# Graph layers by one-hot matmuls: 64 columns in two column groups instead of 32 columns in four

## The chip, the core and the metric

The kernel runs on one NeuronCore of a Trainium2 chip. Its engines are TensorE (PE; its weight loads are listed apart as PEld), VectorE (DVE), ScalarE (ACT), GpSimd (POOL) and SyncE (SP), which run side by side and wait for each other by semaphores. The metric is the device time of one execution in microseconds (us), as the median of several runs.

## The reference

A graph has 3125 nodes with 768 features and 50,000 edges, sorted by their target node. Two layers follow each other, each on a normalised copy of its input and each added to it:

```python
h = relu(layernorm(x)); x = x + conv(relu(conv(h, W1, b1)), W2, b2)   # D^-1/2 (A + I) D^-1/2 h W^T + b
h = relu(layernorm(x)); x = x + attention(h)                          # 12 heads of 64 features
# attention, per head: ft = h W_fc^T; e = leaky(a1[src] + a2[dst]); alpha = softmax of e over the edges of one dst
# relu(sum over edges of alpha * ft[src]  +  h W_res^T)
```

In each of the three passes over the edges (two convolutions, one attention) a node receives the sum of the rows of its source nodes, in attention weighted by alpha.

## The kernel before

**Tiles and gathers.** The nodes are 25 tiles of 128 (the last has 53), and a tile has four units of 32 nodes. The edges of a tile come in quads. A quad holds 17 chunks of 128 edges: four chunks for each unit (512 edges), and one extra chunk whose 128 places are shared by the units. With this input every tile has one quad; the last tile has two units, so a pass makes 24 x 17 + 9 = 417 gathers. A gather is one indirect DMA that POOL issues: it fetches 128 rows (3 KB each, in attention a little more) of a table in DRAM to the 128 partitions of one chunk.

**Sums by one-hots.** For a chunk, DVE makes a 128 x 32 matrix with a one where the edge (partition) goes to the node (column). PE takes it as the stationary operand and the chunk's rows as the moving one, and accumulates in PSUM. As the one-hot has 32 columns, `add` (line 777, matmul at line 779) cuts the 768 features into four strips of 192, each sent to its own group of 32 columns of the array, and so to its own 32 partitions of PSUM: `block_of(par, s, g)` holds for unit s the strip g on partitions 32g to 32g+31. All operands are float32, and each such matmul appears in the trace as two instructions with a weight load each. So a chunk is 8 matmul instructions and a unit 32.

**A convolution** (function `convolution`, run twice). There is one set of 17 chunk buffers, `ring_c`. POOL's `fetch` waits before the four gathers of unit s until PE has used that unit's buffers for the tile before (`unit_done[s]`), and ACT's `next_slot` hands it the row numbers. PE's `step(j)` does, for tile j, the units 0 to 3 as their rows land, the extra chunk (into `ps_x` in natural order of nodes, lines 798), and then the product of tile j-1 with the 768 x 768 weights (line 808, 24 matmul instructions). DVE, for tile j: makes the next one-hots when PE is done with the old ones (lines 833, 836), adds ACT's copy `natural` to the four strips of the four units (16 adds, line 854), waits for the product of tile j-1 (which still reads `sum_t`), transposes in blocks of 32 into `sum_t` (2 transposes, line 860), clears the PSUM half, and finishes tile j-1 (line 875 or 879, 881). Two halves of `ps_sum` alternate between tiles.

**Attention.** Here two sets of chunk buffers alternate, and the order of a tile on each engine is this.
- ACT: `cast_hot` copies the tile's one-hots (bf16) to float32 `hot_f` (line 1344, waits until PE is done with the tile before: `used[3]`); the exponentials that are the edge weights (1368 and 1372, wait for PE's transposes of the scores, line 1472); smaller copies; 36 of 48 scalings of unit 3's rows (line 1388); `sloped` for the next tile (line 1336, waits for PE's `scores`, which end in line 1462); the other 12 scalings; `lay` of the tile before (line 1354): 16 copies of 32 partitions x 192 that bring the result `o` from its strips to natural order in `ps_n`.
- DVE: scales the rows of units 0, 1 and 2 (line 1651, one operation each), between units 1 and 2 takes the terms of the next tile's scores (1562), scales the extra chunk (1658), adds the result of two tiles ago (1580), makes one-hots (1556), then runs the maxima and scans for the next tile (1613 to 1622), then `divide` (1568 to 1574, waits for `used[3]` and, for `o`, for `lay`).
- PE: units 0 and 1 (line 1493, 32 instructions each, each after its scaling), `scores` of the next tile (1455 to 1462), unit 2, the extra chunk for each unit (line 1508, 32 instructions), unit 3 (needs ACT's scalings), transposes, `natural` (the residual product, line 1420).
- POOL: gathers for the tile after next, unit by unit as `used[s]` allows.

When a tile had a second quad, a rescaling of the sums would run; with this input it doesn't.

## Time and profile before

| | |
|---|---|
| time of the runs | median 1934.79 us of 3 (1933.72 to 1936.58) |
| profiled execution, span from first to last instruction | 2277.0 us |
| PE busy | 1621.1 us, 71% |
| POOL busy | 1232.7 us, 54% |
| DVE busy | 1121.9 us, 49% |
| ACT busy | 718.1 us, 32% |
| gathers of the first convolution | begin at 112.2 us |
| gathers of attention | 1531.7 to 2226.3 us |
| mean granted TensorE clock | 0.840 of full |

The page gives no time for what lies around the span of the profiled execution. Its span alone is 342 us longer than the median of the runs, so the profiled execution is not paced as the timed ones are; the rows below have to be read with that in mind. Busy shares are averages over the stages: the part up to 112 us sorts the edges into quads, two convolutions follow, then a dense stage that prepares attention, then attention.

### The profile page before, as it was taken

How to read it: one execution, taken by the hardware profiler on the slowest of the kernel's cores; microseconds unless marked ns; L12 is line 12 of the kernel's file. 1: busy time of each engine (PE TensorE's matmuls, PEld its weight loads, DVE VectorE, ACT ScalarE, POOL GpSimd, SP SyncE). 2: the span in 40 equal slices, each digit the busy share in tenths (PEclk: the TensorE clock that was granted, in tenths of full speed). 3: DMA queues.
4: the chain of work that ended last, by engine and by line, in shares of the span. 5: the costliest groups of instructions: out<-in, count | busy, mean ns of one | idle time of the engine just before them, and what ended most of it. 6: DMA issues, size and time to landing. Idle time of an engine off the chain costs nothing. (4 is left out here: it accounts for less than half of the span.)

```text
span 2277.0 us, 43588 instructions
## 1 busy us (share of the span) xinstructions
PE 1621.1 (71%) x13579; PEld 962.8 (42%) x13580; DVE 1121.9 (49%) x2027; ACT 718.1 (32%) x2184; POOL 1232.7 (54%) x1297
## 2 busy tenths in 40 slices
PE   7337888887778858787788887882666666666665
PEld 7223444444344424344444444671334444444443
DVE  6613334333334314444444444653666666666666
ACT  6400111111111101000000100262666666777675
POOL 2166566566656266566666666106555555555550
PEclk9969888899988869798988888986787777878877
DMA  4698888888878387788787887388788888888882
GB/s 183 218 315 269 268 266 271 274 265 277 275 264 270 125 279 270 261 270 277 262 274 266 266 275 274 122 310 280 245 279 267 270 267 272 273 273 272 273 276 84
DMA packets 139992, 585.22 MB, mean 257 GB/s; under 512 B 30616, under 2 KB 32752, under 8 KB 139946
## 3 DMA queue, kind: packets, MB, share of 16 engines
q0 software_dynamic: 100272, 497.49, 65.7%
q1 hardware_dynamic: 32563, 67.72, 8.6%
q10 hardware_dynamic: 7110, 19.43, 2.2%
q8 instruction: 25, 0.41, 0.1%
q14 instruction: 22, 0.17, 0.0%
HBM read 534.42 MB, written 50.12 MB: 257 GB/s over the span
## 5 line engine op out<-in xcount | busy, mean ns | idle before, releaser
L667 POOL DMA_INDIRECT ring_c<-table,slot_c x834 | 798.1, 957 | 545.9 <-issue 268.5
L1243 POOL DMA_INDIRECT ring<-table,slot x417 | 410.4, 984 | 288.5 <-issue 105.8
L833 DVE TENSOR_TENSOR hots<-iota,units 128x256 f32<-128x256 bf16 x102 | 43.3, 426 | 602.4 <-remote 332.9
L1493 PE MATMUL ps_acc<-ring,hot_f 128*32 128x195 f32 x3136 | 230.8, 386 | 138.2 <-issue 84.4
L1388 ACT ACTIVATE ring<-ring,weight x1152 | 281.5, 340 | 0.6
L1651 DVE TENSOR_TENSOR ring<-ring,ps_w 128x3120 f32 x72 | 244.7, 3398 | 16.5 <-issue 8.9
L1493 PEld LDWEIGHTS ps_acc<-ring,hot_f 128*32 128x32 f32 x3136 | 123.9, 125 | 227.7 <-issue 124.2
L808 PE MATMUL ps_ya<-weights,sum_ta 128*128 128x512 f32 (+1 forms) x576 | 204.1, 503 | 12.5 <-issue 10.9
L808 PE MATMUL ps_yb<-weights,sum_tb 128*128 128x512 f32 (+1 forms) x576 | 196.7, 494 | 6.1 <-issue 5.5
L711 ACT ACTIVATE slot_c<-units 128x8 int32 (+1 forms) x104 | 21.7, 211 | 545.9 <-DMA ring_c<-table,slot_c 391.8
L779 PE MATMUL ps_sum0b<-ring_c,hots 128*32 128x192 f32 x1600 | 136.3, 364 | 75.9 <-issue 66.6
L779 PE MATMUL ps_sum0a<-ring_c,hots 128*32 128x192 f32 x1600 | 123.0, 356 | 75.5 <-issue 46.9
L779 PE MATMUL ps_sum1a<-ring_c,hots 128*32 128x192 f32 x1536 | 125.2, 350 | 63.3 <-issue 57.9
L779 PE MATMUL ps_sum1b<-ring_c,hots 128*32 128x192 f32 x1536 | 125.5, 362 | 61.6 <-issue 60.2
L808 PEld LDWEIGHTS ps_ya<-weights,sum_ta 128*128 128x128 f32 x576 | 113.8, 199 | 104.6 <-issue 95.6
L808 PEld LDWEIGHTS ps_yb<-weights,sum_tb 128*128 128x128 f32 x576 | 112.0, 195 | 90.1 <-issue 81.8
L779 PEld LDWEIGHTS ps_sum0b<-ring_c,hots 128*32 128x32 f32 x1600 | 70.6, 118 | 136.5 <-issue 127.2
L1354 ACT ACTIVATE ps_n<-o_g 32x192 f32<-32x192 f32 x384 | 124.6, 325 | 7.7 <-DVE nodes L1580 3.6
L739 ACT ACTIVATE naturalb<-ps_xb 128x768 f32<-128x768 f32 x25 | 20.3, 812 | 326.8 <-remote 173.8
L739 ACT ACTIVATE naturala<-ps_xa 128x768 f32<-128x768 f32 x25 | 20.3, 812 | 324.2 <-remote 186.0
L779 PEld LDWEIGHTS ps_sum0a<-ring_c,hots 128*32 128x32 f32 x1600 | 66.3, 115 | 127.8 <-issue 106.0
L779 PEld LDWEIGHTS ps_sum1b<-ring_c,hots 128*32 128x32 f32 x1536 | 67.4, 118 | 116.0 <-issue 108.9
(294 smaller groups left out, 2121.0 us busy)
## 6 DMA issues: line engine op xcount, KB each, us to landing
ring_c<-table,slot_c POOLq DMA_INDIRECT x834
table<-ft SPq DMA_DIRECT2D x25, 396.0 KB, 2.8
table<-nodes SPq DMA_DIRECT2D x25, 384.0 KB
table<-nodes ACTq DMA_DIRECT2D x25, 384.0 KB
turned_table<-h_t SPq DMA_DIRECT2D x25, 384.0 KB, 3.0
nodes<-in_x ACTq DMA_DIRECT2D x24, 384.0 KB
turned_g<-turned_table SPq DMA_DIRECT2D x24, 384.0 KB
out_x<-nodes SPq DMA_DIRECT2D x24, 384.0 KB
```

The source lines that it names most:

```text
L667: eng.indirect_dma_start(out=ring[:, t * QH + k, :], out_offset=None, in_=table, in_offset=bass.IndirectOffsetOnAxis(ap=slot[t][:, k:k + 1 ...
L711: eng.activation(slot[t][:, :], units[:, ds(q, 1), t * QH:(t + 1) * QH + t].rearrange("p a c -> p (a c)"), ACT.Copy).then_inc(slot_ready[t ...
L739: eng.activation(natural[:, :], ps_x[:, 0:D], ACT.Copy).then_inc(s_nat, 1)
L779: last = eng.matmul(block_of(par, s, g), hot, rows[:, g * GB:(g + 1) * GB], start=start, stop=True, skip_group_check=True)
L808: last = eng.matmul(product(jj)[:, c0:c0 + n], turned(jj)[:, k, :], w[:, k, c0:c0 + n], start=(k == 0), stop=(k == KB - 1))
L833: eng.tensor_tensor(hots[k][:, :, :].rearrange("p (s c) d -> p s c d", c=CPU), iota0[:, :].unsqueeze(1).unsqueeze(2).to_broadcast([P, 2, C ...
L1243: eng.indirect_dma_start(out=ring[:, b * RB + at * FROW:b * RB + (at + 1) * FROW], out_offset=None, in_=table3, in_offset=bass.IndirectOff ...
L1354: last = eng.activation(ps_n[s * UD:(s + 1) * UD, c0:c0 + GN], o[g * UD:(g + 1) * UD, s, :], ACT.Copy)
L1388: last = eng.activation(head, head, ACT.Copy, scale=weight[:, c, h:h + 1])
L1493: last = eng.matmul(acc_of(s, g), hot_f[:, c, s * UD:(s + 1) * UD], ring[:, x0 + g * GW:x0 + (g + 1) * GW], start=False, stop=True, skip_g ...
L1651: eng.tensor_tensor(mine, mine, given_w[:, 0:CPU, s * H:(s + 1) * H].unsqueeze(3).to_broadcast([P, CPU, H, FH]), ALU.mult).then_inc(scaled ...
```

## The change

Every one-hot of a unit's chunk becomes 64 columns wide: the 32 columns of before beside 32 columns of zeros, so that it addresses a pair of units and adds zero to the partner. The features are cut into two strips of 384 instead of four of 192, and two column groups of 64 are used instead of four of 32.

- Convolutions: `hots` become `pair_hots`, [128, 4 chunks, 3, 32] for each pair of units, with zeros in the middle third; the 64-column window begins at 0 for the even unit and at 32 for the odd one. A chunk is 2 matmuls (4 instructions) of 384 columns. The sums lie on other partitions, so the adds are 4 of 64 x 384 instead of 16 of 32 x 192, and the block transposes are 8 of 32 partitions x 384 instead of 2 of 128 x 384. The zeros are written once.
- Attention: `hot_f` gets the same form and `hot_x` holds the extra chunk's one-hot; `cast_hot` is 3 copies (256, 256 and 128 elements per partition) instead of 1 of 640. Units are 16 instructions instead of 32; the extra chunk is done by pairs, 8 instructions of 390 columns instead of 32 of 195. `lay` is 4 copies of 64 x 384 instead of 16 of 32 x 192, and the adds of the last tile are 2 instead of 8. `divide` works on as many elements as before.

```diff
-                def block_of(par, s, g):
-                    c0 = (s // 2) * 512 + (s % 2) * GB
-                    return ps_sum[par][g * UD:(g + 1) * UD, c0:c0 + GB]
+                def block_of(par, h, g):
+                    return ps_sum[par][g * PW:(g + 1) * PW, h * 512:h * 512 + GC]
+
+                def hot_of(s, c):
+                    return pair_hots[s // 2][:, c, s % 2:s % 2 + 2, :].rearrange("p x d -> p (x d)")
...
-                            for g in range(US):
-                                last = eng.matmul(block_of(par, s, g), hot, rows[:, g * GB:(g + 1) * GB], start=start, stop=True, skip_group_check=True)
+                            for g in range(GP):
+                                last = eng.matmul(block_of(par, s // 2, g), hot, rows[:, g * GC:(g + 1) * GC], start=False, stop=True, skip_group_check=True)
...
-                                for s in range(units_of(j)):
-                                    for g in range(US):
-                                        block_ = block_of(par, s, g)
-                                        last = eng.tensor_tensor(block_, block_, natural[s * UD:(s + 1) * UD, g * GB:(g + 1) * GB], ALU.add)
+                                for h in range(-(-units_of(j) // 2)):
+                                    for g in range(GP):
+                                        block_ = block_of(par, h, g)
+                                        last = eng.tensor_tensor(block_, block_, natural[h * PW:(h + 1) * PW, g * GC:(g + 1) * GC], ALU.add)
...
-                                for b in range(2):
-                                    last = eng.transpose(turned(j)[:, :, b * 2 * UD:(b + 1) * 2 * UD].rearrange("p k (s d) -> p s k d", d=UD),
-                                                         ps_sum[par][:, b * 512:b * 512 + 2 * GB].rearrange("p (s k d) -> p s k d", s=2, d=UD))
+                                for g in range(GP):
+                                    for f in range(2):
+                                        for s in range(2):
+                                            to, of = (g * 2 + f) * UD, (g * 2 + s) * UD
+                                            last = eng.transpose(turned(j)[to:to + UD, :, :].rearrange("p k (h s d) -> p h s k d", h=UP, d=UD)[:, :, s],
+                                                                 ps_sum[par][of:of + UD, :].rearrange("p (h x) -> p h x", h=UP)[:, :, f * GB:(f + 1) * GB].rearrange("p h (k d) -> p h k d", d=UD))
...
-                        eng.activation(hot_f[:, :, :].rearrange("p c e -> p (c e)"), hot[:, ds(par, 1), :, :].rearrange("p a c e -> p (a c e)"), ACT.Copy).then_inc(hot_cast, 1)
+                        given = hot[:, ds(par, 1), :, :]
+                        for t in range(GA):
+                            eng.activation(hot_f[:, t, :, 0:3:2, :], given[:, :, 0:CPU, t * AW:(t + 1) * AW].rearrange("p a c (s d) -> p (a c) s d", d=UD), ACT.Copy)
+                        eng.activation(hot_x[:, :], given[:, :, CPU, :].rearrange("p a e -> p (a e)"), ACT.Copy).then_inc(hot_cast, 1)
...
-                        for g in range(US):
-                            for s in range(US):
-                                c0 = g // 2 * 512 + g % 2 * GN
-                                last = eng.activation(ps_n[s * UD:(s + 1) * UD, c0:c0 + GN], o[g * UD:(g + 1) * UD, s, :], ACT.Copy)
+                        for g in range(GA):
+                            for t in range(GA):
+                                last = eng.activation(ps_n[t * AW:(t + 1) * AW, g * 512:g * 512 + GN], o[g * AW:(g + 1) * AW, t, :], ACT.Copy)
...
-                                    for g in range(US):
-                                        last = eng.matmul(acc_of(s, g), hot_f[:, c, s * UD:(s + 1) * UD], ring[:, x0 + g * GW:x0 + (g + 1) * GW],
+                                    for g in range(GA):
+                                        last = eng.matmul(acc_of(s // UA, g), hot_of(s, c), ring[:, x0 + g * GW:x0 + (g + 1) * GW],
...
-                                for s in range(nu):
-                                    for g in range(US):
-                                        last = eng.matmul(acc_of(s, g), hot_f[:, CPU, s * UD:(s + 1) * UD], ring[:, x0 + g * GW:x0 + (g + 1) * GW],
+                                for t in range(-(-nu // UA)):
+                                    for g in range(GA):
+                                        last = eng.matmul(acc_of(t, g), hot_x[:, t * AW:(t + 1) * AW], ring[:, x0 + g * GW:x0 + (g + 1) * GW],
```

## Rows read from the trace of the kernel before

**Rows 1.** The profile page: the span and the number of instructions.
```profile
span 2277.0 us, 43588 instructions
```

**Rows 2.** Lines 667 and 1243 by themselves: duration min/median/max, first and last start.
```profile
L667 POOL DMA_INDIRECT ring_c<-table,slot_c x834: 943/949/1707, 112.2 to 1435.8; - x167
...
L1243 POOL DMA_INDIRECT ring<-table,slot x417: 943/949/2193, 1531.7 to 2226.3; - x139
```

**Rows 3.** Timeline, first convolution: start, length, what, [idle before, releaser].
```profile
401.17 3.16 PE L779 MATMUL ps_sum0a<-ring_c,hots 128*32 128x192 f32 x70 [0.37 <-issue]
...
402.57 0.95 POOL L667 DMA_INDIRECT ring_c<-table,slot_c  x1 [3.08 <-PE ps_sum0a L779]
...
403.82 0.94 POOL L667 DMA_INDIRECT ring_c<-table,slot_c  x1 [0.30 <-issue]
...
404.63 0.37 PE L779 MATMUL ps_sum0a<-ring_c,hots 128*32 128x192 f32 x2 [0.30 <-issue]
...
414.74 0.95 POOL L667 DMA_INDIRECT ring_c<-table,slot_c  x1 [2.45 <-remote]
```

**Rows 4.** Timeline, the last tile of the first convolution.
```profile
764.84 2.81 PE L779 MATMUL ps_sum0a<-ring_c,hots 128*32 128x192 f32 x64
...
768.97 7.90 PE L808 MATMUL ps_ya<-weights,sum_ta 128*128 128x512 f32 x24
```

**Rows 5.** Groups by line: count | busy, mean ns of one | idle before.
```profile
L1354 ACT ACTIVATE ps_n<-o_g 32x192 f32<-32x192 f32 x384 | 124.6, 325 | 7.7 <-DVE nodes L1580 3.6
...
L854 DVE TENSOR_TENSOR ps_sum0a<-ps_sum0a,naturala 32x192 f32<-32x192 f32 x200 | 73.3, 366 | 6.3 <-ACT naturala L739 2.0 <-issue 1.8
...
L875 DVE SCALAR_TENSOR_TENSOR nodes<-ps_ya,dinv,biases 128x768 f32 (+1 forms) x24 | 24.4, 1018 | 3.5 <-PE ps_ya L808 2.8
...
L715 ACT ACTIVATE ps_xa<-nodes 128x768 f32 (+1 forms) x25 | 20.4, 815 | 10.0 <-PE ps_xa L774 7.4
...
L860 DVE STREAM_TRANSPOSE sum_ta<-ps_sum1a 128x384 f32<-128x384 f32 x24 | 12.6, 562 | 16.1 <-remote 8.4 <-PE ps_ya L808 7.5
```

**Rows 6.** Timeline, a late tile of attention.
```profile
2204.54 0.20 ACT L1372 ACTIVATE weight<-ps_s 128x48 f32<-128x48 f32 x1
...
2211.74 1.53 PE L1493 MATMUL ps_acc<-ring,hot_f 128*32 128x195 f32 x32 [1.90 <-DVE ring L1651]
...
2216.97 0.70 ACT L1336 ACTIVATE top_g<-ps_s 48x640 f32<-48x640 f32 x1 [2.10 <-PE ps_s L1462]
...
2220.45 5.37 ACT L1354 ACTIVATE ps_n<-o_g 32x192 f32<-32x192 f32 x16
2220.50 0.95 POOL L1243 DMA_INDIRECT ring<-table,slot  x1 [4.81 <-PE ps_acc L1508]
2220.60 1.53 PE L1493 MATMUL ps_acc<-ring,hot_f 128*32 128x195 f32 x32 [0.95 <-ACT ring L1388]
...
2223.73 0.48 PE L1472 MATMUL ps_s<-ident,score 48*128 48x48 f32 x5 [1.60 <-DVE score L1622]
...
2226.23 0.74 ACT L1344 ACTIVATE hot_f<-hot 128x640 f32 x1 [0.42 <-issue]
...
2227.00 0.35 ACT L1368 ACTIVATE ps_w<-ps_s 128x240 f32<-128x240 f32 x1
2227.26 0.20 ACT L1372 ACTIVATE weight<-ps_s 128x48 f32<-128x48 f32 x1
...
2231.04 2.83 PE L1493 MATMUL ps_acc<-ring,hot_f 128*32 128x195 f32 x32 [2.15 <-DVE ring L1651]
```

**Rows 7.** The same timeline, one tile later.
```profile
2248.89 0.35 ACT L1368 ACTIVATE ps_w<-ps_s 128x240 f32<-128x240 f32 x1
```

**Rows 8.** Windows: us, busy (count) of PE, PEld, DVE, ACT, POOL, clock, DMA share, GB/s.
```profile
376.40:402.60 26.20, 21.47 (x164) 11.46 (x160) 9.77 (x23) 2.90 (x5) 16.12 (x18) 0.87 0.81 268
2216.90:2219.60 2.70, 2.70 (x64) 1.89 (x64) 2.63 (x5) 2.63 (x10) 0.00 (x0) 1.00 0.69 246
2231.10:2233.80 2.70, 2.70 (x32) 1.31 (x32) 2.70 (x2) 2.70 (x12) 0.00 (x0) 0.50 0.00 0
```

More of the change, by code:

```diff
@@ L54 @@
 GB = D // US
+UP = US // 2
+PW = 2 * UD
+GP = P // PW
+GC = D // GP
 LU = -(-LAST // UD)
@@ L601, in gnn_kernel @@
         ring = sb(by_conv, "ring_c", [P, QC, D])
-        hots = [sb(by_conv, f"hots{k}", [P, n, UD]) for k, n in enumerate((2 * CPU, 2 * CPU, US))]
+        pair_hots = [sb(by_conv, f"pair_hots{h}", [P, CPU, 3, UD]) for h in range(UP)]
+        extra_hot = sb(by_conv, "extra_hot", [P, US, UD])
         slot = [sb(by_conv, f"slot_c{t}", [P, QH + t], I32) for t in range(2)]
@@ L797, in visit @@
                                     for c0, n in HALVES:
-                                        last = eng.matmul(ps_x[:, c0:c0 + n], hots[2][:, :, :].rearrange("p s d -> p (s d)"), ring[:, QX, c0:c0 + n], start=False, stop=True, skip_group_check=True)
+                                        last = eng.matmul(ps_x[:, c0:c0 + n], extra_hot[:, :, :].rearrange("p s d -> p (s d)"), ring[:, QX, c0:c0 + n], start=False, stop=True, skip_group_check=True)
                                     last.then_inc(extra_done, 1)
@@ L1234, in _ @@
                     eng.wait_ge(g_mask, 1)
[L1235 to L1237 removed]
+                    for g in range(GA):
+                        for s in range(UA):
+                            last = eng.affine_select(out=head_of[:, g, s, :, :], in_=head_of[:, g, s, :, :], compare_op=ALU.not_equal, fill=1.0, base=-s * H - g * PR,
+                                                     pattern=[[-UA * H, GA], [-1, PR]], channel_multiplier=1)
                     last.then_inc(g_const, 1)
@@ L1433, in rescale @@
                         eng.sem_inc(passed, 1)
-                        for g in range(US):
-                            last = eng.matmul(ps_l[g * UD:(g + 1) * UD, 64:64 + US * PR], lift[:, :], head_of[:, g, :, :].rearrange("p s k -> p (s k)"), start=True, stop=True)
+                        for g in range(GA):
+                            for s in range(UA):
+                                r0 = g * AW + s * UD
+                                last = eng.matmul(ps_l[r0:r0 + UD, 64:64 + GA * PR], lift[:, :], head_of[:, g, s, :, :].rearrange("p t k -> p (t k)"), start=True, stop=True)
                         last.then_inc(r_all, 1)
@@ L1482, in visit @@
                                     eng.sem_inc(passed, 1)
-                                for s in range(0, US, 2):
-                                    eng.matmul(ps_acc[:, s * 256:s * 256 + 2], ident_b[:, :], nil[:, :], start=True, stop=True, skip_group_check=True)
+                                for t in range(GA):
+                                    eng.matmul(ps_acc[:, t * 512:t * 512 + 2], ident_b[:, :], nil[:, :], start=True, stop=True, skip_group_check=True)
                             with eng.Else():
```

80 lines of the change are left out of this document (43 added, 37 removed).

## The prediction

> **What bounds the kernel now.** Read the page first: the span is 2277.0 us [rows 1], 342 us above the median of the runs, 1934.79. So the first question is what paces the profiled execution and not the timed one. Then I read the gathers' own lines [rows 2]: a gather occupies POOL for 949 ns, and the next starts 0.30 us after it (the gather at 403.82) [rows 3], so POOL issues at best one per 0.949 + 0.30 = 1.25 us. A full tile has 17: 21.3 us. The three passes have 3 x 417 = 1251, which is 1569 us of the 1935.
>
> The timeline of a convolution tile shows that the profiled tile isn't at this floor. It takes 26.2 us (the first window is one tile) [rows 8], and POOL stops twice in it, for 3.08 us for PE and for 2.45 us for something not named, just when PE comes out of a slow stretch [rows 3]. PE had all its rows. It ran 70 matmul instructions in 3.16 us, and then came out at two or three per 0.7 us, idle "for issue" in between, until about 414 us [rows 3]. In other places the same instructions run without a pause: both units of the last tile, 64 instructions, took 2.81 us [rows 4]. The hold comes after long dense runs of PE instructions, it waits for no engine and no rows, and it is in the execution that is 342 us too long. I take it for a cost of recording instructions, which the timed runs don't pay. Check: the 48 full tiles of the convolutions lose 26.2 - 21.3 = 4.9 us each, 235 us. In attention POOL's 417 gathers start over 2226.3 - 1531.7 = 694.6 us [rows 2], or 28.3 us for each of 24.5 tiles, and its last tiles, which happen to be free of the hold, take 2227.26 - 2204.54 = 22.7 and 2248.89 - 2227.00 = 21.9 us [rows 6, 7]. With 22.3 that is 6.0 x 24.5 = 147 us more. Together 382 us, slightly more than the 342. So in the timed runs the convolutions are near POOL's 21.3 us per tile, attention near 22.3, and some 40 us of holds or of slow first tiles remain.
>
> In attention the unheld tile shows what sets the 22.3 us: the loop of ACT. PE's scores release ACT's `sloped` (it waited 2.10 us for them), 12 scalings follow, then `lay` for 5.37 us, then `cast_hot`, then the exponentials at 2227.00, which DVE and the rest of the next tile wait for [rows 6]. POOL stands idle 4.81 us in that tile [rows 6]: it is not the bound there.
>
> **PE in the convolutions.** Array time per column first: 24 instructions of the product (12 of 512 columns, 12 of 256) take 7.90 us [rows 4], 0.857 ns per column. So one instruction of 192 columns is 165 ns, and if four column groups run at once a unit of 32 takes 8 x 165 = 1.32 us; the row says 2.81 for two [rows 4]. They do run at once. After the change a unit is 16 instructions of 384 columns, 329 ns each, two groups at once: 8 x 329 = 2.63 us, 1.31 more. No row has two groups of 64. The bounds are full overlap (2.63) and none (5.26); I take full overlap, as four groups show it. A gain from fewer instructions can't be excluded by bounds alone, but a run of 64 already takes the array's time, so issue adds nothing to take away at this clock.
>
> The Trainium skill speaks against the change: TensorEngine Tiling (Array Packing), section Theoretical Speedup, gives up to 4x for a dimension of 32 and up to 2x for 64. By it the unit is 2.63 us, as by the rows. For it could speak TensorE: Matmul & The Clock Gate (section on the 56 ns gap), where the sequencer may spend about 62 ns per matmul: 32 would take 1.98 us and 16 only 0.99. The row's 44 ns for each instruction is below that, so the rule is not what binds here; by it the loss per unit would be 0.65 instead of 1.31.
>
> A convolution tile on PE: before 4 x 1.32 + 1.32 for the extra chunk (1536 columns at 0.857 ns) + 7.90 = 14.5 us. After: 4 x 2.63 + 1.32 + 7.90 = 19.7, with the starts and ends of the groups about 20.3 us. That is under 21.3, by only 1.0. The order also fits: with the last gather of a tile issued at 0 and some 3 us to land, extra chunk and product fill PE to 12.2 after (12.2 before too), units 0 and 1 are done at 14.9 and 17.5, and POOL needs unit 0's buffers at 21.3. So the cost is 0 as long as the clock is full. What covers it is POOL's own pace; if the cover goes, each us that PE needs above 21.3 costs 48 us in all. Only the two last tiles show it: both units after the last product, +2.6 each, **+5 us**.
>
> **DVE in the convolutions.** Adds: 16 at 366 ns, 5.9 us, become 4 of 384 elements. Between 192 elements (366) and 768 (1018) [rows 5] lies 583 for 384, so 2.3 us: 3.6 less. Transposes: 2 at 562 ns [rows 5] become 8. A quarter of the partitions with 384 elements each may cost the same 562, or as little as a quarter; I take 562, 4.5 us, 3.4 more. They wait for the product of the tile before, and behind them are the clearing, line 875 and the next one-hots; those are wanted by PE only in the next tile, some 15 us later. Zero. The zeros, written once, are below 1 us.
>
> **Attention.** `lay`: ACT's copy costs 325 ns for 192 elements and 815 for 768 [rows 5], so 488 for 384; four make 2.0 us instead of 5.37. `cast_hot`: at the same 0.85 ns per element below its 0.74 us for 640 [rows 6], two of 256 (0.41) and one of 128 (0.30): 1.12, or +0.38. But `cast_hot` waits for `used[3]` as well. Before, unit 3 ended at 2220.60 + 1.53 = 2222.1, long before `lay` did. After, unit 3 takes 1.31 more, ends at 2223.4, and `cast_hot` starts there instead of at 2226.23; the exponentials start at 2224.6 instead of 2227.00. Their other condition, PE's transposes of the scores, is met at 2223.73 + 0.48 = 2224.2 [rows 6]. Gain 2.4 (in the next tile, by the same sum, 2.2).
> Against it: unit 0's extra 1.31 falls into PE's wait of 1.90 for DVE before unit 1 [rows 6]; unit 1's doesn't, so the scores and ACT's `sloped`, which waits 2.10 for them, come 1.3 later. Net 2.3 - 1.3 = 1.0 per tile. The extra chunk keeps its time: 8 rounds of 195 columns before, 4 rounds of 390 after. The two tiles become 21.6 and 20.9 us, but POOL's 21.3 is the floor, so on average 22.3 falls to 21.45: 0.85 x 24 = **-20 us**. The last tile's adds (2 for 8) and its `lay` save about **3 us**. If the real tile before is held up more than 22.3, more is saved, up to 2.2 x 24 = 53.
>
> **Sum:** +5 - 20 - 3 = -18 us, in the profiled execution's terms 2277 to 2259 before the hold is touched, and for the median 1934.8 to **1917 us**. The profile itself should fall far more, since half the recorded PE instructions of the passes go: if the holds vanish, by up to 382 us, to 1900 to 2050.
>
> **The clock.** Rows give the granted clock as 0.50 where 32 instructions take 2.7 to 2.8 us, and 1.00 where 64 take 2.70 [rows 8]: 1.2 and 2.4 GHz. It was down at unit 0 of attention after a stretch in which PE did little, and 0.87 on average over a convolution tile [rows 8]. After the change PE is busy 20 of 21.3 us instead of 14.5, so I expect it to stay up. This is the choice on which most hangs.
>
> **Rivals.**
> - *The holds are partly real* (the 40 us not accounted for are PE holds in the timed runs too). For it: 382 fits 342 only roughly. Then halving the instructions returns up to those 40: 1917 - 40 = 1877, between 1860 and 1895.
> - *Unit 0 at half clock in attention.* The row at 2231.04 shows it: 2.83 us [rows 6]. It starts 3.7 us after the exponentials. After the change it takes 5.3, to 9.0, and unit 1 ends at 11.6; before, unit 1 starts at 7.2 (2211.74 - 2204.54) [rows 6] and ends at 8.7. So the scores come 2.9 later, not 1.3: net 2.3 - 2.9 = -0.6 per tile, a loss of 14 us if in every tile. 1930 to 1955.
> - *PE becomes the bound of the convolutions* (slower). Place: the 48 full tiles of the two convolutions. PE's work is 20.3 us at full clock; it decides once more than 1.0 us of that work runs at half rate. If the clock stays at today's 0.87 [rows 8], a tile takes 20.3 / 0.87 = 23.3, 2.0 over the floor: +98, so 2015. At 0.92 it is 22.1 and +37: 1954. For it: today's clock, and a slack of only 5%. Against: it was low because PE waited, and it will not wait. 1945 to 2015.
> - *The two groups don't overlap.* A unit is 5.26, a convolution tile 30.8 us: over 2350. Against it, four groups do.
>
> **How the numbers follow.** A measurement of this kernel tells a change from none at about 0.2%, 3.9 us. My forecast, 1900 to 1930: 0.46. Holds partly real: 0.14. Half clock in attention: 0.16, of which 0.02 faster, 0.10 within 0.2%, 0.04 slower. PE bound in the convolutions: 0.22. No overlap: 0.02. Faster 0.46 + 0.14 + 0.02 = 0.62; same 0.10; slower 0.04 + 0.22 + 0.02 = 0.28. The range runs from 1870, which leaves about 0.05 of the second case below, to 1985, which leaves about half of the fourth and the fifth above. The forecast alone reaches from 1900 to 1930.
>
> **What the profile after would show.** Units of 16 instructions in 2.6 to 2.8 us. Starts of the same gather 21.3 to 22.5 us apart in the convolutions, without POOL's two stops. `lay` of four copies, 2.0 us, followed by a short wait and `cast_hot`. Clock above 0.95 in the convolutions. Wrong would be: PE without a gap over whole convolution tiles and POOL waiting for it (PE bound), the clock at 0.5 in unit 0 of attention, or ACT waiting more than 4 us for the scores.

## The result, and the profile after

The changed kernel is slightly slower: a median of 1945.16 us in 6 runs (1936.92 to 1958.01) against 1934.26 us for the kernel before in 6 runs (1930.56 to 1936.58), a ratio of 1.007 (95% interval 1.005 to 1.009). The forecast was 1917 us and faster. The profiled execution after took 1936.92 us (span 1935.2), the lowest of its runs, so its rows show less than the 10.9 us between the medians.

The profile of before that stands above, 2277 us long, shows TensorE held in every tile, as on two of the chips of the experiments, where the timed runs of this kernel take 2306 to 2315 us as well; the comparison of 1934 with 1945 is free of that. The rows of the kernel before that stand beside those of after here are therefore from a second profile of it (span 1927.8 us, experiment e16).

The page of after: the span, PE's line and the granted clock in 40 slices.

```profile
span 1935.2 us, 32525 instructions
...
PE 1603.2 (83%) x8287; PEld 853.7 (44%) x8288; DVE 1122.9 (58%) x1736; ACT 644.8 (33%) x1946; POOL 1231.4 (64%) x1297
...
PEclk9979999999999989999999999895989999898999
```

Against [rows 1] there are 11,000 instructions less. The windows say what that did to PE: us, busy time (and count) of PE, PEld, DVE, ACT and POOL, granted clock, DMA share, GB/s. After, a stretch of the first convolution and one of attention:

```profile
171.00:399.00 228.00, 216.10 (x991) 107.45 (x991) 106.47 (x186) 30.82 (x53) 172.54 (x183) 1.00 0.94 331
...
1420.00:1860.00 440.00, 346.44 (x2114) 176.92 (x2112) 347.06 (x315) 312.20 (x1166) 309.03 (x316) 0.95 0.93 327
```

The same stretches of the kernel before, profiled again (e16):

```profile
171.00:399.00 228.00, 175.00 (x1680) 107.50 (x1678) 106.94 (x252) 30.54 (x53) 172.55 (x183) 0.93 0.94 331
...
1420.00:1860.00 440.00, 288.05 (x3728) 196.68 (x3724) 352.76 (x316) 372.26 (x1365) 308.71 (x316) 0.82 0.93 328
```

In the convolution PE is 216 of 228 us busy instead of 175, at full clock instead of 0.93, and POOL makes its 183 gathers in both. In attention PE has 58 us more, ACT 60 us less, and POOL makes the same 316 gathers in 440 us: more of one, less of another, and the same pace.

**Where the 7.4 us between the two profiles are.** The gathers of each pass, with the time of the first and the last; first the two convolutions and attention after, then before (e16).

```profile
L676 POOL DMA_INDIRECT ring_c<-table,slot_c x417: 942/946/1517, 112.2 to 642.9; - x139
...
L676 POOL DMA_INDIRECT ring_c<-table,slot_c x417: 942/946/1727, 677.6 to 1206.4; - x139
...
L1263 POOL DMA_INDIRECT ring<-table,slot x417: 940/946/2197, 1306.3 to 1889.3; - x139
```
```profile
L667 POOL DMA_INDIRECT ring_c<-table,slot_c x417: 942/946/1887, 111.9 to 642.8; - x139
...
L667 POOL DMA_INDIRECT ring_c<-table,slot_c x417: 942/946/1582, 674.5 to 1199.2; - x139
...
L1243 POOL DMA_INDIRECT ring<-table,slot x417: 940/946/2177, 1295.7 to 1878.9; - x139
```

| stretch | before (e16) | after | difference |
|---|---|---|---|
| gathers of the first convolution | 530.9 | 530.7 | 0 |
| last tiles, then the start of the second | 31.7 | 34.7 | +3.0 |
| gathers of the second convolution | 524.7 | 528.8 | +4.1 |
| last tiles, dense stage | 96.5 | 99.9 | +3.4 |
| gathers of attention | 583.2 | 583.0 | 0 |
| end | 48.9 | 45.9 | -3.0 |

In attention the forecast had 20 us less; it is 0 in this pair. One pair of profiles says little about a few us, so here are the same stretches in the other profiles taken where the kernel before takes 1930:

- gathers of attention: 583.2, 581.4 and 579.4 us with attention as before (e16, e4, e1); 583.0, 588.3 and 589.1 with it changed (after, e2, e7). In the mean some 5 us more.
- gathers of the second convolution: 524.7 to 528.2 in six profiles with the convolutions as before, 526.7 to 528.8 in six with them changed. The +4.1 of the table is mostly scatter.
- between the two convolutions: 31.6 to 34.4 against 33.6 to 34.8; before attention: 95.8 to 98.1 against 99.8 to 101.1.

**A convolution tile after.** Timeline of PE: start, length, what, in brackets the idle time before it and who ended it.

```profile
401.22 2.80 PE L788 MATMUL ps_sum0a<-ring_c,pair_hots 128*64 128x384 f32 x16 [1.12 <-DMA ring_c<-table,slot_c]
403.96 1.56 PE L807 MATMUL ps_xa<-ring_c,extra_hot 128*128 128x512 f32 x4
405.35 7.90 PE L817 MATMUL ps_ya<-weights,sum_ta 128*128 128x512 f32 x24
413.18 8.08 PE L788 MATMUL ps_sum1a<-ring_c,pair_hots 128*64 128x384 f32 x48
422.38 0.87 PE L788 MATMUL ps_sum1a<-ring_c,pair_hots 128*64 128x384 f32 x4 [1.11 <-DMA ring_c<-table,slot_c]
```

A unit is 16 instructions in 2.80 us, and 48 in 8.08; the forecast said 2.63 for a unit and 20.3 for the tile (216.1 of 228 us busy is 20.2 of 21.3). From 401.22 to 422.38 PE stops once, for 1.11 us, and it waits for rows to land, not POOL for PE: the cover held, by about the 1.0 us that the forecast gave it.

**A tile of attention after.** The timeline again, with POOL, DVE, ACT and PE:

```profile
1597.26 0.94 POOL L1263 DMA_INDIRECT ring<-table,slot  x1 [0.42 <-issue]
...
1605.56 3.40 DVE L1676 TENSOR_TENSOR ring<-ring,ps_w 128x3120 f32 x1
...
1607.35 0.95 POOL L1263 DMA_INDIRECT ring<-table,slot  x1 [0.30 <-issue]
1609.01 2.84 PE L1517 MATMUL ps_acc<-ring,hot_f 128*64 128x390 f32 x16 [0.59 <-DVE ring L1676]
...
1612.77 0.26 DVE L1587 COPY terms<-ring 128x192 f32 x1 [3.82 <-DMA ring<-table,slot]
...
1613.04 3.40 DVE L1676 TENSOR_TENSOR ring<-ring,ps_w 128x3120 f32 x1
1616.23 0.70 ACT L1356 ACTIVATE top_g<-ps_s 48x640 f32<-48x640 f32 x1 [3.98 <-DVEq L1633]
1616.49 4.50 PE L1517 MATMUL ps_acc<-ring,hot_f 128*64 128x390 f32 x16 [1.96 <-DVE ring L1676]
...
1619.71 1.98 ACT L1376 ACTIVATE ps_n<-o_g 64x384 f32<-64x384 f32 x4
1621.81 1.86 POOL L1263 DMA_INDIRECT ring<-table,slot  x1 [2.87 <-PE ps_acc L1517]
...
1625.14 0.72 ACT L1366 ACTIVATE hot_f<-hot 128x256 f32 x2 [3.46 <-PE ps_acc L1517]
```

`lay` is 1.98 us instead of 5.37 [rows 6], as forecast, but `cast_hot` then waits 3.46 us for unit 3 of PE. DVE has done unit 1's scaling at 1608.96 and stands 3.82 us before `take_terms`: it needs the whole of the next tile's quad, and the last of those gathers was issued at 1607.35. Behind `take_terms` in DVE's queue stands the scaling of unit 2, behind that PE's unit 2, and its end is what POOL waits 2.87 us for. The circle begins where POOL asks for unit 2's buffers, 1597.26, and closes at 1621.81:

1. nine gathers (unit 2, extra chunk, unit 3) until the last is issued: 10.09 us
2. until its rows have landed and DVE takes the terms: 5.42
3. the terms: 0.27
4. DVE scales unit 2: 3.40, and PE begins 0.05 later
5. PE's unit 2: 4.50 here, 2.84 in most tiles
6. until POOL begins: 0.82

Sum 24.55; with 2.84 it would be 22.9. The same steps over 21 tiles of this trace: nine gathers 10.5 on average, landing 5.35, terms 0.28, and from the scaling to POOL's next request 7.55, in all 23.7. In 13 of the 21 the last part is 7.11 to 7.19 (3.40 + 0.05 + 2.84 + 0.82 = 7.11): nothing but this chain. In 5 it is 8.6 to 8.8, where unit 2 takes up to 4.5. In the kernel before (e16) the same part reaches its own shortest, 5.82 or 5.83 (3.40 + 0.05 + 1.53 + 0.82 = 5.80), in 2 of 21 tiles only; otherwise POOL had been held up earlier, at unit 0, as the rows of that kernel show:

```profile
1600.87 0.94 POOL L1243 DMA_INDIRECT ring<-table,slot  x1 [2.88 <-PE ps_acc L1493]
...
1602.46 0.26 DVE L1562 COPY terms<-ring 128x192 f32 x1 [1.89 <-DMA ring<-table,slot]
...
1606.18 1.53 PE L1493 MATMUL ps_acc<-ring,hot_f 128*32 128x195 f32 x32 [1.29 <-DVE ring L1651]
...
1609.53 5.36 ACT L1354 ACTIVATE ps_n<-o_g 32x192 f32<-32x192 f32 x16
...
1610.98 0.95 POOL L1243 DMA_INDIRECT ring<-table,slot  x1 [0.30 <-issue]
...
1615.00 0.96 DVE L1574 TENSOR_TENSOR o_g<-ps_acc,rden 128x768 f32<-128x768 f32 x1 [1.21 <-ACT ps_n L1354]
```

The same can be read from POOL's idle time before its first request of a unit, which is 0.30 us when nothing holds it. Averages over 19 tiles of attention, from the starts of its gathers:

| | before unit 0's gathers | before unit 2's gathers |
|---|---|---|
| before (e16) | 2.21 | 0.33 |
| after | 1.29 | 1.15 |
| e3, changed, terms late | 1.10 | 0.33 |
| e6, before, short `lay` | 0.83 | 1.22 |
| e5, changed, half columns | 0.85 | 1.06 |
| e17 and e18, both cuts | 0.46 and 0.34 | 0.39 and 0.30 |

Before the change POOL is held once per tile, at unit 0; after it, less there and a second time at unit 2. (The runs e3 to e18 are told below.)

The waits in 440 us of attention (1420 to 1860) say the same. Columns: who waits for whom, us in total, times, longest. After:

```profile
ACT top_g L1356 <- DVEq L1633: 82.4, 18, 6.2
DVE terms L1587 <- DMA ring<-table,slot: 82.3, 19, 6.0
```

Before (e16):

```profile
ACT top_g L1336 <- DVEq L1608: 47.8, 15, 4.0
DVE terms L1562 <- DMA ring<-table,slot: 47.6, 18, 3.6
...
DVE o_g L1574 <- ACT ps_n L1354: 21.9, 19, 1.2
```

The wait for `lay` is gone, and DVE's wait for the landing of the next tile's rows has grown by 35 us.

### The profile page after: what moved, and what is told of

Read it like the earlier page. It is cut to its first block and busy times, and to the rows that moved or that the text cites. A ratio compares the mean times of both kernels' runs of the same rounds, so it can differ in the third digit from the quotient of the medians.

```text
span 1935.2 us, 32525 instructions
## 1 busy us (share of the span) xinstructions
PE 1603.2 (83%) x8287; PEld 853.7 (44%) x8288; DVE 1122.9 (58%) x1736; ACT 644.8 (33%) x1946; POOL 1231.4 (64%) x1297
## 5 line engine op out<-in xcount | busy, mean ns | idle before, releaser
L1517 PE MATMUL ps_acc<-ring,hot_f 128*64 128x390 f32 x1568 | 301.6, 533 | 79.0 <-DVE ring L1676 76.3
L1517 PEld LDWEIGHTS ps_acc<-ring,hot_f 128*64 128x64 f32 x1568 | 117.2, 147 | 233.2 <-issue 133.9
L788 PE MATMUL ps_sum0a<-ring_c,pair_hots 128*64 128x384 f32 x800 | 141.7, 504 | 36.7 <-DMA ring_c<-table,slot_c 36.5
L788 PE MATMUL ps_sum0b<-ring_c,pair_hots 128*64 128x384 f32 x800 | 140.0, 500 | 24.6 <-DMA ring_c<-table,slot_c 24.6
L788 PE MATMUL ps_sum1b<-ring_c,pair_hots 128*64 128x384 f32 x768 | 133.8, 499 | 23.7 <-DMA ring_c<-table,slot_c 23.7
L788 PE MATMUL ps_sum1a<-ring_c,pair_hots 128*64 128x384 f32 x768 | 131.0, 490 | 17.8 <-DMA ring_c<-table,slot_c 17.7
L788 PEld LDWEIGHTS ps_sum0a<-ring_c,pair_hots 128*64 128x64 f32 x800 | 60.6, 141 | 113.5 <-issue 80.5
L788 PEld LDWEIGHTS ps_sum0b<-ring_c,pair_hots 128*64 128x64 f32 x800 | 59.5, 139 | 100.2 <-issue 77.7
L788 PEld LDWEIGHTS ps_sum1b<-ring_c,pair_hots 128*64 128x64 f32 x768 | 57.2, 139 | 95.8 <-issue 79.6
L788 PEld LDWEIGHTS ps_sum1a<-ring_c,pair_hots 128*64 128x64 f32 x768 | 56.6, 137 | 88.2 <-issue 69.7
```

Of the source, the lines that this page charges most:

```text
L788: last = eng.matmul(block_of(par, s // 2, g), hot, rows[:, g * GC:(g + 1) * GC], start=False, stop=True, skip_group_check=True)
L1517: last = eng.matmul(acc_of(s // UA, g), hot_of(s, c), ring[:, x0 + g * GW:x0 + (g + 1) * GW], start=False, stop=True, skip_group_check=True)
```

## The experiments

Five series, each on another chip, each with runs of the kernel before on the same chip: 1931.46 us (e1 to e4), 1932.63 (e5 to e8), 2311.25 (e9 to e11), 2312.96 (e12 to e15), 1932.86 (e16 to e18). Ratios are against those. The changed kernel itself ran in one of them only (e14); where a run is set against its 1945.16 us, the two are from different series, whose kernels before differ by up to 3 us.

**e1 and e2: one part alone.** e1 has the hunks of the diff in the convolutions, e2 those in attention.

> Only the convolutions are changed, attention stays with 32 columns. Theory A (the loss is attention's: POOL paces the convolutions at 21.3 us per tile and hides the longer matmuls): the time stays within 0.4% of before, 1934 to 1941 us, the last tiles adding about 5 us. Theory B (the loss comes from the convolutions, where PE has 20.3 of 21.3 us to do): slower by 8 us or more, and attention alone would then be no slower than before.

> Only attention is changed. Theory A (a loop in attention through the buffers: PE is done with unit 2, POOL asks for unit 2, the extra chunk and unit 3 of a later tile, they land, DVE takes the terms, scales unit 2, PE does unit 2; each unit on PE is 1.3 us longer and so is the loop): slower than before by 6 to 30 us, as much as the whole change or nearly. Theory B (the convolutions lose, and attention gains by its shorter copies): faster than before, by up to 20 us.

e1: 1938.9 us, ratio 1.0039 (1.0023 to 1.0055). e2: 1940.32 us, 1.0047 (1.0028 to 1.0067). Both lie where the expectation that blames attention had them, but the convolutions have their share: 7.5 and 9 us. The sum, 16.5, is above the 10.9 of the whole change; with these intervals that is no contradiction, and the shares are known to some 4 us only. In e1's profile the gap between the two convolutions' gathers is 33.6 us and that before attention 100.7; in e4, with the convolutions of before, 31.9 and 95.8. Together +6.6, where the forecast had +5.

**e3 and e4: the terms later.** The changed kernel (e3) and the kernel before (e4), with DVE taking the next tile's terms behind unit 2's scaling instead of ahead of it.

```diff
-                                if s == early_of(j) - 1:
+                                if s == nu - 2:
                                     take_terms(q + 1)
```

> The whole change, and DVE takes the terms of the next tile after it has scaled unit 2 instead of before; nothing else moves. The loop then goes landed, terms 0.5, scores 1.3, unit 2 on PE 2.8, without the 3.4 us of scaling in it. Theory A (that loop sets attention's 23.6 us per tile): the tile falls to 21.4 to 22.3 us, and the time by 30 to 50 us, to 1895 to 1915. Rival (the DMA engines, busy 92 to 95% of the time in attention, set the pace; the wait for landed rows is only where it shows): the time stays within 10 us of the changed kernel.

> The same move of the terms in the kernel before. Theory A (before the change the loop was about 22.3 us and ACT's own loop with the long copies 21.9 to 22.7): little is gained, 0 to 20 us, since ACT's loop takes over; 1915 to 1935. Rival (DMA load): within 5 us of before.

e3: 1918.78 us, 0.9934 (0.9916 to 0.9951), 24 to 26 us less than the changed kernel. That is short of the 30 to 50 us of theory A and well beyond the 10 us of its rival, the DMA engines: their busy share in the 440 us is 0.93 after and 0.95 in e3, at 327 and 339 GB/s, so they weren't at their limit in the changed kernel. e4: 1930.45, 0.9991 (0.9978 to 1.0004), nothing; this lies within both of its expectations and separates nothing by itself. The waits of e3:

```profile
ACT top_g L1356 <- DVEq L1633: 88.7, 19, 6.5
...
POOL ring L1263 <- PE ps_acc L1517: 23.5, 22, 2.7
...
DVE terms L1587 <- DMA ring<-table,slot: 19.3, 10, 3.0
```

and those of e4:

```profile
DVE o_g L1574 <- ACT ps_n L1354: 53.1, 19, 3.0
POOL ring L1243 <- PE ps_acc L1493: 40.4, 28, 3.4
```

ACT's wait for its top scores (88.7 us) is as long as in the changed kernel while the time fell, so its length tells nothing of what binds. What the edit takes out is the 3.40 us of scaling behind the landing, and not the landing itself: in PE's own queue the next tile's scores, which need the terms, stand ahead of unit 2. In e3:

```profile
1627.60 0.26 DVE L1587 COPY terms<-ring 128x192 f32 x1 [0.23 <-issue]
...
1629.12 1.15 PE L1486 MATMUL ps_s<-ident,terms 128*48 128x128 f32 x9
...
1630.21 2.78 PE L1517 MATMUL ps_acc<-ring,hot_f 128*64 128x390 f32 x15
```

DVE had scaled unit 2 by 1627.37, and PE begins it at 1630.21, behind the scores. With the scaling out of that chain, the kernel before is left with the other one: `divide` waits 53.1 us for `lay`, and POOL is still held 2.05 us at unit 0.

**e5: half of the columns.** In the changed kernel each matmul of a unit in attention moves 195 of the 390 columns, so half of the units' sums are left out and a unit takes 1.54 us instead of 2.84.

```diff
-    last = eng.matmul(acc_of(s // UA, g), hot_of(s, c), ring[:, x0 + g * GW:x0 + (g + 1) * GW],
+    last = eng.matmul(acc_of(s // UA, g)[:, 0:GW // 2], hot_of(s, c), ring[:, x0 + g * GW:x0 + g * GW + GW // 2],
```

> The changed kernel with the attention units' matmuls on 195 of their 390 columns: 16 instructions at about half of the 2.84 us, so some 1.4 us less of TensorE for each unit. The other half of the units' sums is left out; gathers, scalings, extra chunk, lay and divide are as in the changed kernel. Theory of the release loop (unit 2's buffers are given back, POOL asks for nine chunks, they land, VectorE scales unit 2, TensorE multiplies it and gives them back): the loop is 1.4 shorter, 23.8 us per tile become about 22.4, 24 x 1.4 = 34 less than the changed kernel's 1940 to 1945, so 1906 to 1920. Rival, VectorE and ScalarE set the tile and TensorE's length has no part: within 5 us of the changed kernel. Rival, the prediction's loop through ScalarE with only the scores late by one unit: also up to 1.4 per tile, but then the waits of POOL for used buffers would stay as they are and ScalarE's wait for the scores would shrink.

1919.75 us, 0.9937 (0.9914 to 0.9959): 25 us less than the changed kernel's 1945, at the weak end of what the release loop expected, and outside its first rival. POOL's wait for used buffers in 440 us fell from 42.8 us to 28.8, and ACT's for its top scores from 82.4 to 74.9 only; the second rival expected POOL's wait unchanged and ACT's to shrink. So the longer units cost about 25 us. In this run the granted clock in attention fell from 0.95 to 0.87, and 15 of 92 units took 2.87 us, as 20 of 96 took 2.83 in the kernel before: it has the units of before, slow ones included.

**e6: a short `lay` in the kernel before.** Only the first of the four copies of each strip (`for s in range(1)` for `for s in range(US)`), so three quarters of the result in natural order are left out.

> The kernel before with 4 of the 16 copies of lay, so that lay takes about 1.4 us instead of 5.37. Three quarters of the result's way to natural order are left out. The prediction's loop through ScalarE (lay, then cast_hot and the exponentials) expects a tile 4.0 us shorter down to POOL's floor of 21.3: from 22.3, 24 us less than the kernel before's 1931 to 1935, from 23.6 up to 50 less, so 1880 to 1910. The release loop through unit 2 expects that lay matters only through VectorE's and TensorE's waits for it: 0 to 12 less, 1920 to 1935.

1914.36 us, 0.9906 (0.9879 to 0.9933): 18 us less. That lies between the two expectations, 0 to 12 and 24 to 50, and neither had it: `lay` was in a chain that bound, for part of its length.

**e7: `lay` in 16 pieces in the changed kernel.** Each copy cut into four of 96 columns.

```diff
+    for z in range(0, GN, 96):
-        last = eng.activation(ps_n[t * AW:(t + 1) * AW, g * 512:g * 512 + GN], o[g * AW:(g + 1) * AW, t, :], ACT.Copy)
+        last = eng.activation(ps_n[t * AW:(t + 1) * AW, g * 512 + z:g * 512 + z + 96], o[g * AW:(g + 1) * AW, t, z:z + 96], ACT.Copy)
```

> The changed kernel with each of the 4 copies of lay cut into 4 of 96 columns, 16 copies of an estimated 0.25 us, so lay takes about 3.9 us instead of 1.98; nothing is left out. The prediction's loop through ScalarE expects 1.9 us more per tile where lay ends later than unit 3: up to 24 x 1.9 = 46 more than the changed kernel, 1960 to 1990. The release loop through unit 2 expects lay hidden behind TensorE's unit 3, for which cast_hot waits anyway: 0 to 10 more, 1940 to 1955.

1944.52 us, where the changed kernel took 1945.16. A single copy took 234 ns in the median, but the 16 in a row 3.08 us, so `lay` was 1.1 us longer than the changed kernel's 1.98 and not the expected 1.9. Against the kernel before the ratio is 1.0068 (1.0042 to 1.0095), beside 1.007: no cost is seen. `cast_hot` waits for PE's unit 3, and its wait fell from 36.8 us to 18.9 in the 440 us: what `lay` lost, the wait gave.

**e8: the attention part alone, with late terms.**

> The attention part of the change alone, with the convolutions as before, and VectorE taking the terms of the next tile after unit 2's scaling instead of before it. If the order of VectorE takes the landing of the terms out of the release loop, and the convolutions' cost is the two last tiles' 6.6 us, this is the changed kernel with the late terms (1918.8) less 6.6: 1912, between 1908 and 1916, faster than both kernels by 1.0 to 1.3 per cent. Rival, the gain of the late terms needs the changed convolutions (a different state of the queue or of TensorE's clock when attention begins): 1925 or more.

1915.37 us, 0.9916 (0.9896 to 0.9937), as the theory said (1908 to 1916). Of the kernels that leave nothing out it is the fastest, 17 us below the kernel before.

**e9: the kernel before, once more.**

> The kernel before once more, unchanged, for its profile. If the stalls of TensorE in the profiled execution of 2277.0 us are what recording this kernel's 43588 instructions costs, as the prediction put it, they come again: a span over 2200 and convolution tiles of 26 us. If they belonged to that one execution, the span is 1925 to 1945, the gathers of the convolutions stand 21.3 us apart per tile, and attention shows VectorE's divide waiting for lay in nearly every tile (53 us in 19 waits in the kernel before with late terms) beside VectorE's wait for the terms to land (under 60 us).

The span was 2308.3 us and the convolution tiles stood 26.5 us apart, as the first reading expects, and yet all 13 timed runs of the kernel before on that chip took 2305.99 to 2315.3 us. There the hold is in the timed runs as well; e16 settles it.

**e10 and e11, e12 and e13, e17 and e18: both cuts together.** e10 is e6 with late terms (three quarters of `lay` left out), e11 is e5 with late terms (half of the units' sums left out). The first two pairs ran where the kernel before takes 2310, the third where it takes 1930.

> The kernel before with 4 of the 16 copies of lay (three quarters of it left out) and VectorE taking the next tile's terms after unit 2's scaling. In the kernel before two loops of nearly equal length take turns, one through lay and one through the landing of the terms: alone, the late terms gave nothing (1930.5) and the short lay 18 us (1914.4). If so, both together give more than their sum: the changed kernel with late terms in attention alone (1915.4) has the same two cuts and units 1.3 us longer, so this one should be up to 24 x 1.3 = 31 below it: 1885 to 1905. Rival: once both cuts are made, TensorE's unit length has no part and what binds is the chain from the terms to the next tile's weights: 1908 to 1916.

> The changed kernel with the units' matmuls on 195 of 390 columns (half of the units' sums left out) and VectorE taking the next tile's terms after unit 2's scaling. Alone, the half columns gave 25 us and the late terms 26. If both cut the same loop and POOL's 21.3 us per tile is not reached (tiles were 23.2 and 23.0), together they give 30 to 50 of 1945: 1895 to 1915. Rival: after the late terms TensorE's units are no longer in the loop that binds: 1914 to 1920.

> As e10, in a new series; three quarters of lay are left out. Where the kernel before takes 1930 to 1936: theory of two loops of nearly equal length, and TensorE's unit in both, 1885 to 1905; rival, TensorE's unit has no part once both cuts are made, 1908 to 1916. Where the kernel before takes about 2310, TensorE's holds bind and this kernel is within 0.2 per cent of it, as in e10.

> As e11, in a new series; half of the units' sums in attention are left out. Where the kernel before takes 1930 to 1936: 1895 to 1912 if half columns and late terms cut the release loop one after the other; 1914 to 1920 if TensorE's units are no longer in the loop that binds after the late terms. Where the kernel before takes about 2310: 0.96 to 0.97 of it, as in e11.

> As e10, three quarters of lay left out. On a chip of the 1930 kind: 1885 to 1905 if TensorE's unit is in the loop that then binds (the changed kernel with late terms in attention alone took 1915.4 with units 1.3 us longer), 1908 to 1916 if it has no part. On a chip of the 2310 kind: within 0.2 per cent of the kernel before, as e10 and e12.

> As e11, half of the units' sums in attention left out. On a chip of the 1930 kind: 1895 to 1912 if half columns and late terms shorten the same loop one after the other, 1914 to 1920 if TensorE's units are no longer in the loop that binds. On a chip of the 2310 kind: 0.966 of the kernel before, as e11 and e13.

e17: 1895.29 us, 0.9803 (0.9773 to 0.9832). e18: 1893.24 us, 0.9792 (0.9764 to 0.982). In the kernel before, late terms alone gave 1 us and the short `lay` 18, both together 38: two chains of nearly equal length, of which one takes over when the other is cut. e17 lies in the expected 1885 to 1905; e18 is 2 us below the expected 1895 to 1912. In e17 POOL hardly waits for PE any more (waits in the same 440 us):

```profile
POOL ring L1243 <- PE ps_acc L1508: 4.7, 1, 4.7
...
POOL ring L1243 <- PE ps_acc L1493: 3.4, 11, 0.3
```

Its gathers take 548.3 us in e17 and 542.5 in e18, 22.4 and 22.1 per tile, against the floor of 21.3. Against e3 (late terms, units of 2.84 us) e18 differs by the half columns alone and takes 25.5 us less; against e8 e17 has shorter units and a `lay` shorter by 0.7 us and takes 20 less. So PE's unit still counts when the terms are taken late, as the first expectation had it. Where the kernel before takes 2310, e10 and e12 were 0.9994 (0.9979 to 1.0008) and 0.999 (0.9977 to 1.0003), e11 and e13 0.9661 (0.9619 to 0.9704) and 0.9662 (0.9638 to 0.9686); these four say nothing of which chain binds at 1930.

**e14 and e15: the changed kernel where PE is held.**

> The changed kernel itself. Where the kernel before takes 1930 to 1936: 1.005 to 1.009 of it, as in the first comparison. Where it takes about 2310 and TensorE is held in every tile: if a hold goes with the number of TensorE's instructions, 0.95 to 0.98 of it, since the passes have 13579 instructions before and about half of the units' after; if it goes with TensorE's busy time, 1.02 or more, since the units take 1.3 us more each.

> The changed kernel with the terms taken late. Where the kernel before takes 1930 to 1936: 0.992 to 0.995 of it, as in e3. Where it takes about 2310: within 0.3 per cent of e14, since there TensorE's holds bind and not VectorE's order.

e14: 2293.39 us, 0.9929 (0.9887 to 0.997). e15: 2290.44, 0.991 (0.9885 to 0.9934). There the change makes the kernel faster. Neither of e14's two readings of the hold fits: by instructions it would have been 0.95 to 0.98, by busy time over 1.02. In attention the late terms gave nothing there (0.1 per cent, within the intervals) while half of the columns took 55 us off e15 (e13, 2235.68).

**e16: the kernel before where it takes 1930.**

> The kernel before, unchanged, for its profile. On a chip of the 1930 kind: a span of 1925 to 1940, the gathers of the convolutions 21.3 us apart per tile, attention's gathers over 575 to 585 us (23.5 to 23.9 per tile), VectorE waiting for lay before divide in nearly every tile and for the terms' landing in some. On a chip of the 2310 kind: as e9.

Span 1927.8 us with the same 43588 instructions as in e9, so the hold is no cost of recording; and all that was expected: 21.3 us per convolution tile, 583.2 us of attention, `divide` waiting for `lay` 19 times (21.9 us in all) and the terms' landing (47.6). Its rows stand in the section on the result.

## Why the prediction was wrong

**The step that failed** is the one in which attention's tile was costed: "It is not the bound there" of POOL, and behind it "Net 2.3 - 1.3 = 1.0 per tile", 20 us of gain. What the runs show for its two terms: the 1.3 per tile (31 us) cost about 25 (e5), and the 2.3, cut by POOL's floor, gave back at most 18 (e6, whose `lay` is shorter by 4.0 us). So the net is a loss of about 7 us. POOL's own work wasn't the bound, but its 4.81 us of idle time [rows 6] was not slack; that row names its releaser, PE. A ring of buffers that is full closes a loop: used, asked for, landed, scaled, multiplied, used. The forecast followed only ACT's loop and took PE's extra 1.3 us as a delay of the scores. It left out that `take_terms` stands ahead of unit 2's scaling in DVE's queue and waits for the last gather of the tile, which puts 5.35 us of landing and PE's unit 2 into one chain with POOL's nine gathers. Before, with e16's averages for the gathers, the landing and the terms and the shortest last one, this chain is 10.3 + 5.8 + 0.3 + 5.8 = 22.2 us: shorter than the 23.8 of the tile, so it did not bind, but by less than `lay` could give back. With 1.3 more for unit 2, and the five tiles in which it is longer still, it is the 23.7 that the 21 tiles show.

e5 says it from the other side: the whole change with the unit times of before is 13 us faster than the kernel before. The 7 us are near e2's 9; the forecast had -23 there (20 and the 3 of the end). That the gain stops where the second chain takes over is shown by POOL's holds (e6: 2.21 to 0.83 at unit 0, 0.33 to 1.22 at unit 2) and by e4, e6 and e17 together.

**The tile of 22.3 us as the start** was wrong too. It was read from two tiles at the end of a held execution, and POOL's last gather of all starts at 2226.3 [rows 2], between them: in such tiles the loop through the buffers is at its end. e16 shows 583.2 / 24.5 = 23.8 us, and there too the last tile is shorter, 21.5 us between the last two starts of line 1368.

**The holds** were read as a cost of recording instructions. e9 and e16 refute it: the same 43588 instructions are recorded in 2308.3 us and in 1927.8, and the timed runs of each chip agree with its profile. The arithmetic of that paragraph was right (48 tiles by 4.9 us, and 147 us in attention), its cause not. The rival "holds are partly real" has nothing for it at 1930: there half of the convolutions' tiles or more are within 0.3 us of 21.3 in both kernels. Where the kernel before takes 2310 it is real, and there the change does gain (e14). A slip on the way: 1251 gathers at 1.25 us are 1564 us and not 1569; nothing rests on it.

**The convolutions** went as forecast. A full tile stays at 21.3 us in the first and 21.4 to 21.5 in the second (medians); PE at 2.80 us per unit and full clock keeps under it, by about as little as was said. The transposes take 579 ns each, the upper of the two bounds, and stay hidden in full tiles. The two last tiles cost 3.0 + 3.4 = 6.4 us here and 6.6 in e1, forecast +5. The second convolution's 4.1 us in this pair were not forecast; over twelve profiles it is some 1.6, within their scatter.

**The clock**, "the choice on which most hangs", came out right: 1.00 in a stretch of either convolution (171 to 399 and 720 to 1200 us) where before had 0.93 in both. The rival "PE becomes the bound of the convolutions" did not come.

**Sizes in attention** were right: `lay` 1.98 us (forecast 2.0), the casts 0.72 + 0.29 = 1.01 (1.12), a unit 2.84 of 390 columns and 2.80 of 384 (2.63). That two column groups of 64 run at the same time follows from 2.80, where one after the other would give the forecast's 5.26. By the Trainium skill, TensorEngine Tiling (Array Packing), section Theoretical Speedup, 64 columns gain up to two times and 32 up to four; the trace agrees, 2.84 against 1.53 us for the same rows.

**The rival "unit 0 at half clock"** is refuted in its form. Unit 0 took 2.83 us before, in the rows of e16 as in [rows 6], at half clock (granted 0.50 from 1597.20 to 1600.00 in e16), and 2.84 after at full clock (1.00 from 1605.60 to 1608.40): the clock gave back there what the wider columns cost. A low clock showed at unit 2 instead: four units that stand alone in the timeline took 4.3 to 4.5 us, and in the one of the tile shown (1616.50 to 1620.99) the granted clock was 0.62. Its time, 1930 to 1955, is where the result lies, but for another reason, so the number is no support for it.

**The end** saved 3.0 us, as forecast (3).

**The signs of being wrong** that the prediction named: the first two did not show; the third did, ACT waited for the scores 4.6 us on average (82.4 us in 18 waits) and up to 6.2. It pointed at attention, but not at the cause: e3 has the same wait and is 24 to 26 us faster.

What stays open: which chain holds e3 at 1918.8, where a shorter `lay` is already in and the scaling is out of unit 2's chain. POOL is held there at unit 0 (1.10 us) and no longer at unit 2, and e18 shows that PE's units are part of it; the full circle wasn't worked out. And what holds PE where the kernel takes 2310.

## What to carry to other kernels

An engine that waits for buffers is part of a loop, and its idle time is no slack: add up the whole circle, from asking for a buffer over landing, scaling and use to giving it back, with every instruction that stands ahead in the same queue, before an edit that lengthens one member of it. When two chains are nearly equal, the gain of cutting one is read from both cut together; one alone can show little (1 us for the late terms here, 18 for the short `lay`, 38 for both), while what an edit adds to the other is paid nearly in full (25 us of 31). If the profiled execution is far from the median, profile it again, on another chip too, before explaining the difference.

## What the runs showed of the hardware

The same program took 1925 to 1940 us in every run on three chips and 2306 to 2315 in every run on two others. Each chip was met in one series only, so whether this belongs to the chip or to its condition at that hour isn't shown. Where it takes 2310, PE is held in every tile. The timeline of PE in a convolution tile of e9 (kernel before):

```profile
457.25 3.12 PE L779 MATMUL ps_sum0a<-ring_c,hots 128*32 128x192 f32 x68 [0.39 <-issue]
460.66 0.36 PE L779 MATMUL ps_sum0a<-ring_c,hots 128*32 128x192 f32 x2 [0.28 <-issue]
461.42 0.52 PE L779 MATMUL ps_sum0a<-ring_c,hots 128*32 128x192 f32 x4 [0.41 <-issue]
```

and of the changed kernel, e14:

```profile
447.34 1.50 PE L788 MATMUL ps_sum0a<-ring_c,pair_hots 128*64 128x384 f32 x7
450.46 0.48 PE L788 MATMUL ps_sum0a<-ring_c,pair_hots 128*64 128x384 f32 x1 [1.61 <-issue]
453.99 8.27 PE L788 MATMUL ps_sum0a<-ring_c,pair_hots 128*64 128x384 f32 x34 [3.05 <-issue]
```

PE stands idle with nothing named that it waits for, in e14 from 448.9 to 450.4 us at a granted clock of 1.00. The stretches of e9 and e14, same columns as above:

```profile
171.00:399.00 228.00, 184.39 (x1288) 95.84 (x1286) 83.15 (x199) 24.81 (x42) 139.23 (x148) 0.83 0.80 266
```
```profile
171.00:399.00 228.00, 194.57 (x791) 94.44 (x792) 81.62 (x144) 24.82 (x42) 141.25 (x149) 0.92 0.80 271
```

148 gathers against 183 in the same time. There the change shortens the gathers of each convolution (654.5 and 649.9 us to 638.4 and 633.6) and lengthens attention's (705.1 to 714.4). So the sign of this change depends on where it runs: 1.007 in the one condition, 0.993 in the other. Why PE is held, and by what rule, these runs don't tell.
